# A gated cross-attention and mixture-of-experts block: stacked attention rows adjacent and without zero rows, loaded in four groups of two batches, maxima rows sent by ScalarE

## What is computed

```python
q = layernorm(x) @ Wq ; kv = concat(ctx, layernorm(x)) @ Wkv
dots = einsum(q, k) * d ** -0.5          # 8 batches, 16 heads, 256 x 320
dots = where(j > i + 64, -inf, dots) ; attn = softmax(dots)
x = x + tanh(g_xattn) * (attn @ v @ Wout + bout)
```

## Time and profile before

| | |
|---|---|
| median of 3 executions | 278.56 us |
| the profiled execution, device time | 278.96 us |
| its span | 277.2 us |
| mean granted TensorE clock | 0.948 of 2.4 GHz |
| TensorE matmuls busy | 228.3 us (82% of the span) |
| VectorE, ScalarE, GpSimd busy | 157.7, 134.1, 160.7 us |
| moved by DMA | 24.93 MB in 31157 packets |

### The profile page before, as it was taken

The page is one execution under the profiler, slowest core; times in us unless marked ns, Lnnn a source line. Parts: engine busy times, 40 slices in busy tenths (PEclk is TensorE's granted clock), DMA queues, the critical chain, the costliest instruction groups (busy, mean ns, idle before and its releaser), DMA issues.

```text
span 277.2 us, 6040 instructions
## 1 busy us (share of the span) xinstructions
PE 228.3 (82%) x2233; PEld 145.1 (52%) x2233; DVE 157.7 (57%) x444; ACT 134.1 (48%) x300; POOL 160.7 (58%) x248
## 2 busy tenths in 40 slices
PE   1699968189999999999999999749899999999600
PEld 1587414045666666666666655424466666666400
DVE  6689884236888888888898655530034333433400
ACT  6277205137788786777787774330133333333100
POOL 5665693414756597877868743777004455666552
PEclk9999997858999999999999999997999999999965
DMA  7564388987232234243200020121463556562220
GB/s 197 81 111 114 105 113 97 121 221 169 62 92 73 62 89 121 91 152 121 60 14 22 11 68 12 38 69 41 105 172 79 114 119 140 134 137 26 18 20 5
DMA packets 31157, 24.93 MB, mean 90 GB/s; under 512 B 3859, under 2 KB 28312, under 8 KB 31128
## 3 DMA queue, kind: packets, MB, share of 16 engines
q1 hardware_dynamic: 25536, 19.23, 29.5%
q0 software_dynamic: 4352, 4.71, 9.4%
q10 hardware_dynamic: 1240, 0.61, 0.8%
HBM read 9.27 MB, written 5.82 MB: 54 GB/s over the span
## 4 chain that ended last, share of the span: by engine, by line
PE 57%; DVE 10%; POOL 9%; DMA 9%; issue 7%; ACT 4%; POOLq 1%; SPq 0%; DVEq 0%
PE PS L1209 12%; PE PS L1189 7%; PE PS L1377 7%; PE PS L1379 6%; DMA qst<-mrow 6%; PE PS L1388 6%; POOL places L669 4%; DVE mxb L919 3%; ACT pt L766 3%; PE PS L1148 2%; PE PS L1173 2%; PE PS L1242 2%; PE PS L1165 2%; PE PS L1168 2%; PE PS L1367 1%
## 5 line engine op out<-in xcount | busy, mean ns | idle before, releaser
L766 ACT ACTIVATE pt<-PS 128x512 f32<-128x512 f32 x128 | 71.3, 596 | 40.2 <-PE PS L1189 39.2
L1189 PE MATMUL PS<-qst,kst 64*128 64x192 bf16 (+2 forms) x384 | 48.7, 242 | 14.1 <-DMA qst<-mrow 10.6
L705 POOL DMA_INDIRECT out<-kst x24 | 36.4, 1516 | 41.2 <-DMA out<-kst 18.9
L919 DVE TENSOR_REDUCE mxb<-PS 128x2 bf16<-128x640 f32 x64 | 52.1, 815 | 0.0
L918 DVE TENSOR_REDUCE mxb<-PS 128x2 bf16<-128x384 f32 x64 | 34.8, 543 | 24.9 <-PE PS L1173 24.4
L1189 PEld LDWEIGHTS PS<-qst,kst 64*128 64x128 bf16 x384 | 30.2, 96 | 35.3 <-DMA qst<-mrow 11.6
L1081 DVE TENSOR_TENSOR kst<-PS,kst 128x320 f32<-128x320 f32 x32 | 15.7, 491 | 49.7 <-ACT kst L851 49.7
L669 POOL DMA_INDIRECT places<-rows,dest x32 | 33.1, 1034 | 16.0 <-issue 9.3
L1209 PE MATMUL PS<-pt,vp 128*32 128x256 f32 (+2 forms) x768 | 38.7, 321 | 0.6 <-DVE pt L1040 0.5
L628 POOL TENSOR_SCALAR_AFFINE_SELECT pt<-pt 128x512 f32<-128x512 f32 x28 | 19.0, 677 | 31.2 <-ACT pt L766 31.1
L1148 PE MATMUL PS<-ones 128*128 128x512 bf16 x102 | 28.9, 408 | 0.0
(11 more groups left out here) (141 smaller groups left out, 369.7 us busy)
## 6 DMA issues: line engine op xcount, KB each, us to landing
kp<-in_w SPq DMA_DIRECT2D x24, 256.0 KB, 2.9
kst<-kp SPq DMA_DIRECT2D x18, 160.0 KB, 3.6
qst<-qp SPq DMA_DIRECT2D x18, 128.0 KB, 3.5
places<-blank POOLq DMA_DIRECT2D x8, 162.5 KB, 5.1
kst<-places SPq DMA_DIRECT2D x8, 130.0 KB, 2.4
out<-xs SPq DMA_DIRECT2D x4, 256.0 KB, 2.7
kst<-kp SPq DMA_DIRECT2D x12, 80.0 KB, 2.1
qst<-qp SPq DMA_DIRECT2D x12, 64.0 KB, 2.1
```

Source lines behind the costliest of these rows:

```text
L705: nc.gpsimd.indirect_dma_start(out=tokens, out_offset=bass.IndirectOffsetOnAxis(ap=ex[0:n, e, s, D:D + 1].bitcast(u32), axis=0), in_=yr[0: ...
L766: nc.scalar.activation(pt[:, U % 2, h, :], PS[:, 4 + h % 2, :], ACT.Exp, scale=SCALE).then_inc(exp_done, 1)
L919: nc.vector.tensor_reduce(mxb[:, U % 2, 1, :, p], PS[:, a:a + 2, 192:512], axis=AX.X, op=ALU.max).then_inc(max_done, 1)
L1189: c = nc.tensor.matmul(PS[:, 4 + par, c0:c1], keys_of(r, gp)[:, g0 + p, i, k0:k0 + 128], queries_of(r, gp)[:, g0 + p, i, q0:N], start=True ...
```

## The change

The three parts of one row of the stack become adjacent: partition 64 par + 8 r + c. One parity is then 48 adjacent partitions (six rows of 8 elements), with the maximum on partition 64 par + 48. The scores contract over 48 partitions, the transposed scores over 49; there are no zero rows. A row of the six is no longer one strided slice of both parities, so each load becomes two DMAs, one per parity, from 64 partitions to 8. The minus ones become two DMAs of one partition per group. The stacks get groups of their own, four of two batches. The maxima of a unit are two DMAs, one per parity, from 4 partitions to 1, and ScalarE issues them for all 16 units. SyncE's loop has no wait for the maxima any more. GpSimd issues four of group 0's 24 loads. Core of the diff:

```diff
+    STACKS = tuple((b, 2) for b in range(0, B, 2))
-    SPAN, MROW, ZROW = 8, 6, 7
+    QROW = 6 * HD
+    KROWS = QROW + 1
-        minus = sb("minus", [2 * HD, 512], bf16)
+        minus = sb("minus", [1, KEYS], bf16)
         def place(U):
-            return GROUP_OF[b], b - GROUPS[GROUP_OF[b]][0], UP * (U % 2)
+            return b // 2, b % 2, UP * (U % 2)
-        def load_q(eng, g, r):
-            b0, n = GROUPS[g]
+        def load_q(eng, g, par, r, landed):
+            row = 64 * par + HD * r
+            b0, n = STACKS[g]
             eng.wait_ge((q1_done, q2_done, q3_done)[QPART[r]], b0 + n)
-            eng.dma_start(queries_of(rows_of(r), g).rearrange("p g b n -> p g (b n)"),
-                          qp[:, QPART[r], b0:b0 + n, :].rearrange("p b n -> p (b n)")).then_inc(stack_in[g], 16)
+            eng.dma_start(queries_of(slice(row, row + HD), g).rearrange("p g b n -> p g (b n)"),
+                          qp[64 * par:64 * par + 64, QPART[r], b0:b0 + n, :].rearrange("p b n -> p (b n)")
+                          ).then_inc(landed, 16)
...
         def load_maxima(eng, U):
-            eng.dma_start(queries_of(slice(MROW, 128, SPAN * HD), gp)[:, g0:g0 + UP, i, :],
-                          mrow[:, U % 2, :]).then_inc(m_in[U % 2], 16)
+            for par in range(2):
+                row = 64 * par + QROW
+                eng.dma_start(queries_of(slice(row, row + 1), gp)[:, g0:g0 + UP, i, :],
+                              mrow[UP * par:UP * par + UP, U % 2, :]).then_inc(m_in[U % 2], 16)
         def stacked(eng, g):
-            eng.wait_ge(stack_in[g], 16 * 12)
-            eng.wait_ge(fixed_in[g >= 2], 16 * 4)
+            eng.wait_ge(stack_in[g], 16 * (24 if g else 20))
+            if g == 0:
+                eng.wait_ge(stack_pool, 16 * 4)
...
-            def load_fixed(i):
+            def load_minus(g):
+                b0, n = STACKS[g]
+                for par in range(2):
+                    mn = minus[:, :]
+                    sp.dma_start(kst[64 * par + QROW:64 * par + KROWS, b0 * PAIRS * KEYS:(b0 + n) * PAIRS * KEYS]
+                                 .rearrange("p (a k) -> p a k", k=KEYS),
+                                 bass.AP(tensor=mn.tensor, offset=mn.offset,
+                                         ap=[mn.ap[0], [0, n * PAIRS], [1, KEYS]])).then_inc(fixed_in[g], 16)
...
             for tick in range(UNITS):
-                if BY_ACT <= tick + 1 < UNITS:
-                    load_maxima(sp, tick + 1)
-                if tick == 0:
-                    load_quarter(sp, 2, 3)
-                elif tick < 9:
-                    load_quarter(sp, 3 + (tick - 1) // 4, (tick - 1) % 4)
+                if tick < 8:
+                    load_quarter(sp, 2 + tick // 4, tick % 4)
+                    if tick % 4 == 1:
+                        load_minus(2 + tick // 4)
...
             third_parts(0)
             rstd_of(3)
+            third_parts(1)
             rstd_of(4)
-            third_parts(1)
+            load_part(pool, load_q, QPART, 0, 1, stack_pool)
...
                 nc.scalar.copy(mrow[:, U % 2, :], MT).then_inc(mrow_done, 1)
-                if U < BY_ACT:
-                    load_maxima(act, U)
+                load_maxima(act, U)
...
-                if p == 0 and U % 2 == 0 and i == 0:
+                if p == 0 and U % 4 == 0:
                     stacked(pe, gp)
-                    heads.append((PS[:, a + par, :], slice(64 * par, 64 * par + 64), slice(64 * par, 64 * par + 64)))
+                    heads.append((PS[:, a + par, :], slice(64 * par, 64 * par + QROW), slice(64 * par, 64 * par + 64)))
...
-                r = slice(64 * par, 64 * par + 64)
+                r = slice(64 * par, 64 * par + KROWS)
```

More of the change, by code:

```diff
@@ L189, in flamingo_gated_block @@
         vp_set = sem("vp_set")
-        fixed_in = [sem(f"fixed_in{i}") for i in range(2)]
+        fixed_in = [sem(f"fixed_in{g}") for g in range(len(STACKS))]
         consts = sem("consts")
@@ L215, in flamingo_gated_block @@
         v_done = sem("v_done")
-        stack_in = [sem(f"stack_in{g}") for g in range(len(GROUPS))]
+        stack_in = [sem(f"stack_in{g}") for g in range(len(STACKS))]
+        stack_pool = sem("stack_pool")
         s_ready = sem("s_ready")
@@ L374, in place, with load_k, load_part @@
             b = U // 2
-            return GROUP_OF[b], b - GROUPS[GROUP_OF[b]][0], UP * (U % 2)
+            return b // 2, b % 2, UP * (U % 2)
         places = nc.dram_tensor("places", (SLOTS, ROW), fp32, kind="Internal").ap()
         block = es.enter_context(nc.Block())
-        def rows_of(r):
-            return slice(r, 128, SPAN)
-        def load_q(eng, g, r):
-            b0, n = GROUPS[g]
+        def load_q(eng, g, par, r, landed):
+            row = 64 * par + HD * r
+            b0, n = STACKS[g]
             eng.wait_ge((q1_done, q2_done, q3_done)[QPART[r]], b0 + n)
-            eng.dma_start(queries_of(rows_of(r), g).rearrange("p g b n -> p g (b n)"),
-                          qp[:, QPART[r], b0:b0 + n, :].rearrange("p b n -> p (b n)")).then_inc(stack_in[g], 16)
-        def load_k(eng, g, r):
-            b0, n = GROUPS[g]
+            eng.dma_start(queries_of(slice(row, row + HD), g).rearrange("p g b n -> p g (b n)"),
+                          qp[64 * par:64 * par + 64, QPART[r], b0:b0 + n, :].rearrange("p b n -> p (b n)")
+                          ).then_inc(landed, 16)
+        def load_k(eng, g, par, r, landed):
+            row = 64 * par + HD * r
+            b0, n = STACKS[g]
             eng.wait_ge((k1_done, k2_done, k3_done)[KPART[r]], b0 + n)
-            eng.dma_start(keys_of(rows_of(r), g).rearrange("p g b k -> p g (b k)"),
-                          kp[:, KPART[r], b0:b0 + n, :].rearrange("p b k -> p (b k)")).then_inc(stack_in[g], 16)
-        def load_part(eng, load, parts_, g, part):
+            eng.dma_start(keys_of(slice(row, row + HD), g).rearrange("p g b k -> p g (b k)"),
+                          kp[64 * par:64 * par + 64, KPART[r], b0:b0 + n, :].rearrange("p b k -> p (b k)")
+                          ).then_inc(landed, 16)
+        def load_part(eng, load, parts_, g, part, landed):
             for r in range(6):
                 if parts_[r] == part:
-                    load(eng, g, r)
+                    load(eng, g, 0, r, landed)
+                    load(eng, g, 1, r, landed)
         def load_quarter(eng, g, quarter):
@@ L402, in load_quarter @@
             for part in ((0,), (1, 2))[quarter % 2]:
-                load_part(eng, load, parts_, g, part)
+                load_part(eng, load, parts_, g, part, stack_in[g])
         def load_maxima(eng, U):
@@ L463, in load_expert @@
+            sp.wait_ge(consts, 4)
+            load_minus(0)
+            load_part(sp, load_q, QPART, 0, 0, stack_in[0])
+            load_part(sp, load_k, KPART, 0, 0, stack_in[0])
+            load_part(sp, load_k, KPART, 0, 1, stack_in[0])
+            load_part(sp, load_q, QPART, 0, 2, stack_in[0])
+            load_part(sp, load_k, KPART, 0, 2, stack_in[0])
+            load_minus(1)
+            for quarter in (0, 2, 1, 3):
+                load_quarter(sp, 1, quarter)
             def load_expert(e):
@@ L519, in _ @@
             nc.gpsimd.memset(half[:, :], -0.5).then_inc(consts, 1)
-            nc.gpsimd.memset(minus[:, :], 0.0).then_inc(consts, 1)
-            for i in range(2):
-                pool.wait_ge(consts, 4 + i)
-                nc.gpsimd.affine_select(out=minus[:, :], in_=minus[:, :], compare_op=ALU.not_equal, fill=-1.0,
-                                        base=-HD * i, pattern=[[0, 512]], channel_multiplier=1).then_inc(consts, 1)
+            nc.gpsimd.memset(minus[:, :], -1.0).then_inc(consts, 1)
             def rstd_of(g):
```

46 lines of the change are left out of this document (15 added, 31 removed).

## The result

The changed kernel takes 297.63 us (median of 4, 295.36 to 303.34), the one before 278.61 (4, 277.73 to 279.78) on the same chip: a ratio of 1.065, 95% interval 1.054 to 1.076. The direction was forecast, and 297.6 lies in the range of 273.5 to 300, near its upper end; the point, 288.0, was 9.6 us short.

The account below looks back on a forecast made before the run. TensorE, busy for 82% of the span, was taken as the bound, with its stalls. Terms of -10.7, +6.8, +10.0 and +3.4 sum to +9.5 us, giving 288 us beside the median of 278.56; range 273.5 to 300.

Parts of the forecast that it names:

- the late start: Group 0's loads onto neighbouring partitions take 126 ns a packet and land at 40.3 us: a loss of 10.0 us.
- 54 GB/s: Rate of a new load reaching two ports by the SBUF page alone: 1.2 and 1.5 us a load, an estimate of 300 us.
- the fills go: Without SyncE's large fills the maxima land in 2.6 us, early stalls and slow clock go: 10.7 us gained by unit 4.
- Rival 4: The stream of loads takes the fills' place in delaying units 0 and 1's maxima: 284 us, chance 0.03.
- the clock's return: At unit 1, no stall and no slow clock: 6.5 us for 14.00, a gain of 7.5 us.
- ScalarE's issues: Two maxima issues a unit on ScalarE, units 4 to 15, delay exponentials and row writes: 6.8 us lost, between 0 and 13.8.
- The wait for group 1: Group 1's loads land at 67.4 us, unit 4's first scores want them at 64.1: a wait of 3.4 us.
- full crowding: Loads take 157 ns a packet without overlap, group 0 lands at 46 and group 1 at 80: 301 us, chance 0.17.

Follow-up runs that it names:

- a1: The changed kernel with the 8 rows of each load on partitions 6 apart instead of adjacent: 277.22 us, ratio 0.975 to the kernel before.
- d2: The changed kernel with each load's 8 rows on partitions 2 apart, in every group: 278.31 us, ratio 0.977 to the kernel before.
- d3: The changed kernel with each load's 8 rows on partitions 3 apart, in every group: 278.99 us, ratio 0.983 to the kernel before.
- c1: The changed kernel with loads onto partitions 6 apart and both rows of maxima in one DMA by ScalarE: 274.35 us, ratio 0.963 to the kernel before.
- a0: The changed kernel run again as it is, on another chip: 300.33 us, ratio 1.050 to the kernel before.
- b0: The kernel before, run again unchanged on another chip: 283.94 us, ratio 0.999.
- a3: The changed kernel with loads onto partitions 6 apart and SyncE sending the maxima from unit 4 on: 277.92 us, ratio 0.973 to the kernel before.

## Why the prediction was right, and where it was short

**Direction and the late start: right.** The step was that loads onto 8 neighbours crowd, at 126 ns a packet, between 60 and 157. The windows give 111 ns at 22 to 30 us and 83 at 30 to 38 us (16 x 0.56 / 111), so the 126 was 14 to 52% too high. First scores were to come at 40.3 and came at 37.84, +7.6 us for +10.0. That the cause is the neighbours is shown by a1, d2 and d3.

The page SBUF — State Buffer of the Trainium skill (Door 1: The DMA port swizzle) gives a DMA 27.2 GB/s for each port that its partitions reach, four neighbours to a port. By it two loads of 8 neighbours, one in each half, reach four ports, an estimate of 109 GB/s; two of 8 rows two apart reach eight, 218. The traces agree with that in part: 93 to 111 with neighbours between 22 and 38 us, 152 where the loads ask for no more, and 219 and 223 for the kernel before's loads over eight ports; but the 133 and the 78 with neighbours are well off 109, so that the ports are an explanation that fits the direction and is not shown as the mechanism. By the formula of that page of the Trainium skill 8 rows 6 apart reach six or seven ports, not the eight that d2's expectation gives them; this changes nothing here, since an estimate of 218 for two loads of rows 2 apart is already above the 152 asked for. The prediction's 54 GB/s by the same page of the Trainium skill took one load at a time; every rate measured with neighbours here is above it. The page DMA: Bandwidth & Descriptors of the Trainium skill (Rules for kernel authors) advises one transfer of 128 partitions over two to disjoint halves, as these serialize. a1, c1, d2 and d3 keep the two and are all faster than before, so here the halves were not what cost; one transfer of all rows was not tried.

**The step that failed: "the fills go", -10.7.** It put the landing of the maxima at the median of the key loads before, 2.6 us, and called 0 its lower end, to be had "if the landings stayed as slow". They stayed slow: 5.8, 9.1 and 7.1 us (6.1, 4.5 and 7.8 in a0). The four ticks cost 4.2 us more in the first pair of profiles and 2.1 less in the second, where 10.7 less was forecast; with the tick behind them it is 7.0 and 2.0 us more. So what came is near or above the lower end. Rival 4 had named it, at a chance of 0.03, on the ground that unit 2's DMA was not waited for at 219 GB/s. But those were loads spread over 16 partitions 8 apart. In the same text I let the new loads crowd at the start and took them as harmless for the maxima behind them; the one assumption forbids the other. With the loads apart, the term is about right: a1 takes 25.7 us for the four ticks that took 37.85 before and 36.09 in b0, 12.1 and 10.3 less.

**Clock, uncounted.** The long waits are followed by stretches at a lower granted clock (0.72 behind the first scores, 0.61 to 0.83 up to unit 4's copy), where a1, after a wait of 1 us, stays at 1.00. The tick behind has 0.70 without a wait for a DMA in it and is 2.8 us too long; in a0 it has a wait of 3.3 us. The prediction counted the clock's return as a gain at unit 1 and its loss nowhere: in the first profile at least the +1.3 and the +2.8 of the table are this.

**ScalarE's issues: near in size, wrong in kind.** 6.8 us were forecast from unit 4 to 15 and 7.6 came from unit 5's copy on (4.8 in the second pair). In ticks at full clock it is 0.41 us where 0.3 was forecast, and 0.80 and 0.58 where 0.84 was (8.31 for 7.51, 8.30 for 7.72). At these prices the ten ticks would come to 4.9 to 6.0 us, an estimate; the rest of the 7.6 are three ticks of 9.15 or 9.16 us, at a clock of 0.81, so that the nearness to 6.8 is partly luck. And c1 shows that all of the 0.4 is the second DMA of each pair, a3 that it is gone when SyncE sends both.

**The wait for group 1, +3.4: absent.** Each load was taken as serial on one queue at 1.0 to 1.26 us; they overlap, and issue goes on at 0.65 us a load. No wait for a stack load stands behind the first scores. That the units themselves ran late helped, so this term and the one that failed were not independent.

**Sum.** +10.0, -10.7, +6.8, +3.4 became +7.6, +4.2, +7.6 and 0, with 1.3, 2.8 and 0.7 beside them: 24.1 us against 9.5 in the profiled executions, 19.0 between the medians. The time lies in the range because the range reached up to full crowding, not because the terms held: the late start did, and ScalarE's nearly, the largest gain failed, and one loss did not come.

## What to carry to other kernels

When a DMA puts few partitions into a stack, look at the partitions it touches on both sides before its size or its count: loads onto rows two or more apart went as fast as they were issued here, 152 GB/s, and onto neighbours at 93, and the order of stacked rows is free to choose. A small DMA on which the tensor engine waits suffers from a crowded stream in flight, though another engine issues that stream (here ScalarE's maxima beside SyncE's loads); and an issue that looks like a burden on a busy queue may be what paces that stream, so look what runs ahead once it is moved. Once nothing crowds, the change as such is worth no more than leaving it out: c1, without zero rows, is at 0.963 of before, and b1, before with its fills read from rows apart, at 0.962.

## What the runs showed of the hardware that I had not expected

- A fill that reads 16 neighbouring partitions and writes 16 partitions 8 apart is slowed by its source alone: 157 ns a packet of 1024 bytes, 72 with the source spread.
- Two apart was enough for this stream: 93 GB/s at 1 apart, then 152, 154 and 154 at 2, 3 and 6 apart, in the stretch from 22 to 30 us, where no more is asked for.
- Loads onto neighbours crowd at a DMA share little above one half (0.63 and 0.56 at 93 and 111 GB/s, 0.56 at 133, 0.59 at 78), with the maxima DMAs at 5.8 to 9.1 us from issue to landing; a1's first ticks have 0.42 to 0.53, and the maxima DMA in its chain took 2.2 us. A share of one half was no sign of spare room.
- One DMA of 4 KB for the maxima by ScalarE was free in the ticks that write no rows; two of 2 KB cost 0.4 us in each of them, and nothing when SyncE issued them.
- The ticks that write a batch's rows took 7.77 us on the first chip and 8.58 on another, for the same kernel before at full clock; this stays open.
